# Idle transposes at both ends of the many-head cross attention of a 32-batch perceiver on one core

## What is computed

```python
x = x + _L2_xattn_ref(_layernorm(x, axis=-1), ctx_1024, ctx_1024, mask_1x1xSxS2_bk1,
                      L2_xattn_W_q, L2_xattn_W_k, L2_xattn_W_v, L2_xattn_W_o)

Q = _split(query @ W_q.T)
K = _split(key @ W_k.T)
V = _split(value @ W_v.T)
scores = jnp.einsum('bhqd,bhkd->bhqk', Q, K) / jnp.sqrt(jnp.float32(D_K))
scores = jnp.where(mask, -jnp.inf, scores)
attn_w = jax.nn.softmax(scores, axis=-1)
...
return merged @ W_o.T
```

## Time and profile before

| | us |
|---|---|
| median of 3 runs | 3170.89 (3170.31 to 3174.92) |
| the profiled execution | 3176.26 |
| its span, from the first to the last instruction | 3174.5 |
| mean granted clock of TensorE in it | 0.901 |
| PE busy | 2655.7 (84%) |
| DVE busy | 2031.4 (64%) |
| ACT busy | 1385.5 (44%) |

### The profile page before, as it was taken

The page is one execution under the profiler, slowest core; times in us unless marked ns, Lnnn a source line. Parts: engine busy times, 40 slices in busy tenths (PEclk is TensorE's granted clock), DMA queues, the critical chain, the costliest instruction groups (busy, mean ns, idle before and its releaser), DMA issues. The chain is left out here.

```text
span 3174.5 us, 65839 instructions
## 1 busy us (share of the span) xinstructions
PE 2655.7 (84%) x26678; PEld 1702.4 (54%) x26678; DVE 2031.4 (64%) x6795; ACT 1385.5 (44%) x2527; POOL 427.0 (13%) x299
## 2 busy tenths in 40 slices
PE   7989553796999699999999999999947989988433
PEld 5767442454666445665556556566524555655323
DVE  5554303576111259899989998998557876536776
ACT  3441211464333225555555555555338964335411
POOL 0000101341000000000000000000004950554100
PEclk9989786897999769999999999999768999899766
DMA  7960041000000100001000100010002210990000
GB/s 238 333 206 1 26 133 29 8 3 16 14 14 14 39 22 23 23 23 33 23 23 23 33 23 23 23 33 2 1 8 80 97 54 6 334 352 26 9 0 14
DMA packets 78239, 188.98 MB, mean 60 GB/s; under 512 B 12418, under 2 KB 46149, under 8 KB 77904
## 3 DMA queue, kind: packets, MB, share of 16 engines
q1 hardware_dynamic: 76912, 182.91, 17.5%
q0 software_dynamic: 1024, 1.85, 0.2%
HBM read 154.19 MB, written 30.79 MB: 58 GB/s over the span
## 5 line engine op out<-in xcount | busy, mean ns | idle before, releaser
L3031 DVE CUSTOM_DVE_ANT_0 L_xattn_junk<-L_xattn_ps_mx,L_xattn_shift 128x512 f32<-128x512 f32 (+1 forms) x1024 | 544.9, 570 | 127.3 <-issue 117.2
L3112 ACT ACTIVATE L_xattn_pT<-L_xattn_ps_st 128x512 f32<-128x512 f32 x768 | 416.9, 594 | 412.4 <-PE L_xattn_ps_st L2882 412.4
L2895 PE MATMUL L_xattn_ps_mx<-L_xattn_kT,L_xattn_qb 32*128 32x512 f32 (+1 forms) x2048 | 496.4, 567 | 1.8 <-DVE L_xattn_tops L3031 1.8
L2882 PE MATMUL L_xattn_ps_st<-L_xattn_qb,L_xattn_kT 32*128 32x256 f32 (+1 forms) x3328 | 463.4, 389 | 0.0
L3077 DVE TENSOR_TENSOR L_xattn_pT<-L_xattn_pT,L_xattn_capT 128x512 f32<-128x512 f32 (+1 forms) x704 | 419.3, 637 | 40.5 <-ACT L_xattn_pT L3112 37.8
L2882 PEld LDWEIGHTS L_xattn_ps_st<-L_xattn_qb,L_xattn_kT 32*128 32x128 f32 (+1 forms) x3328 | 304.1, 183 | 20.7 <-issue 1.2
L2942 PE MATMUL L_xattn_ps_pv<-L_xattn_pT,L_xattn_v 128*17 128x128 f32 x6656 | 267.7, 280 | 0.0
L2942 PEld LDWEIGHTS L_xattn_ps_pv<-L_xattn_pT,L_xattn_v 128*17 128x17 f32 x6656 | 148.4, 98 | 167.0 <-issue 81.0
L2908 PE MATMUL L_xattn_ps_st<-L_xattn_less,L_xattn_ones_b 3*128 3x512 bf16 x768 | 180.6, 390 | 1.4 <-ACT L_xattn_pT L3112 1.2
L1882 DVE SCALAR_TENSOR_TENSOR x<-L_ffn_ps_o,L_ffn_weights,x 128x128 f32<-128x128 f32 x128 | 36.1, 345 | 224.4 <-PE L_ffn_ps_o L1795 224.4
L2895 PEld LDWEIGHTS L_xattn_ps_mx<-L_xattn_kT,L_xattn_qb 32*128 32x128 f32 x2048 | 157.8, 188 | 36.0 <-DVE L_xattn_tops L3031 23.5
(11 more groups left out here) (611 smaller groups left out, 4974.5 us busy)
## 6 DMA issues: line engine op xcount, KB each, us to landing
L_xattn_ctxT<-context_turned SPq DMA_DIRECT2D x64, 800.5 KB, 5.9
L_xattn_ctx<-in_ctx SPq DMA_DIRECT2D x64, 768.0 KB
context_turned<-L_xattn_ctxT SPq DMA_DIRECT2D x32, 800.5 KB, 9.6
L_attn_cc<-scratch_rows SPq DMA_DIRECT2D x32, 512.0 KB, 3.7
L_ffn_w<-in_L_ffn_w SPq DMA_DIRECT2D x32, 256.0 KB, 3.2
L_xattn_out_keys<-scratch_q SPq DMA_DIRECT2D x32, 200.1 KB, 10.0
L_ffn_w<-in_L_ffn_W SPq DMA_DIRECT2D x16, 256.0 KB, 3.1
L_xattn_mask<-in_mask_pairs SPq DMA_DIRECT2D x32, 100.1 KB, 15.1
```

Source lines behind the costliest of these rows:

```text
L2882: last = nc.tensor.matmul(st[0:chunk[j], w % 3, 256 * c2:256 * c2 + 256], kT[n % 3][r:r + 32, P * j:P * j + chunk[j]], qb[n % 3][r:r + 32, ...
L2895: last = nc.tensor.matmul(mx[:, w % 3, to:to + width], qb[n % 3][32 * g:32 * g + 32, 2 * (p % 2):2 * (p % 2) + 2, :].rearrange("p h q -> p ...
L3031: last = nc.vector.tensor_tensor_reduce(out=junk[:, w % 3, to:to + width], in0=mx[:, w % 3, to:to + width], in1=shift[:, k0:k0 + width], s ...
L3112: nc.scalar.activation(pT[b % HELD][:, :, gi, :], st[:, w % 3, :].rearrange("p (c k) -> p c k", c=2), ACT.Exp)\
```

## The change

Three things, all in `many_head_cross_attention`. `masked_here` no longer names bundles from BUNDLES - LEAD = 430 on: the masks of bundles 438, 441 and 443 go from PE (line 2921) to DVE (line 3077), and the waits that count them follow, since all engines ask the same function. A new function on PE, `kept_busy`, called at the end of each iteration, transposes the identity into a part of a bank that nobody reads: 8 times in each of the 14 iterations before -18, 6 times in each of the 18 iterations -18 to -1 (into `st`, not in use before iteration 0), and 4 times in each of the 27 iterations 431 to 457 (into `mx`). Ahead of the last sort stands one new wait, in iteration 431, until DVE has taken all maxima out of `mx`.

```diff
-        masked_here = lambda b: b % ROUND in ON_TENSOR
+        masked_here = lambda b: b % ROUND in ON_TENSOR and b < BUNDLES - LEAD
...
+            def kept_busy(b):
+
+                if b < 0:
+                    for _ in range(8 if b < -LEAD else 6):
+                        nc.tensor.transpose(st[:, 2, 0:P], c.ident[:, :], c.ident[:, :])
+                elif b > BUNDLES - LEAD:
+                    if b == BUNDLES - LEAD + 1:
+                        pe.wait_ge(topped, 2 * BUNDLES)
+                    for _ in range(4):
+                        nc.tensor.transpose(mx[:, 0, 0:P], c.ident[:, :], c.ident[:, :])
+
             for b in range(FIRST, LAST):
...
                 prepare(early(b))
                 prepare(late(b))
+                kept_busy(b)
```

## The result

The change is faster, by less than forecast. Its median is 3154.2 us (7 runs, 3150.2 to 3162.5), and the ratio to the kernel before, run beside it (median 3177.4 us of 7), is 0.9936 (95% interval 0.9925 to 0.9946), which is 20 us; run once more later it was 0.9954 (0.9939 to 0.9969), 15 us. The forecast was 29.4 us. One slow execution of the kernel before (3692 us, mean granted clock 0.691) is left out of every comparison. The trace has a span of 3152.4 us in place of 3174.5, and its mean granted clock went from 0.901 to 0.921.

A forecast was written before the change was run, and what follows sets the result against it. TensorE at half clock was taken to bound both ends of the many-head stage. Terms of +2.5 - 15.2 - 1.2 - 15.5 = -29.4 us took the median from 3170.9 to 3141.5 us, range 3132 to 3157.

The forecast's parts named there:

- A: Both ends of the many-head stage run at full clock; 3141.5 us expected, 3133 to 3150, chance 0.80.
- D: In the fill the clock rises but falls again among the narrow maxima for some 20 us; 3156 us, chance 0.06.
- What bounds the two ends: Fill and drain of the many-head stage are set by TensorE at half clock, not by idleness; at most 57 us available.
- Fill, first part: Iterations -32 to -19, 8 transposes each: the clock rises after 3 to 6 us; 20.6 us against 18.1, costs 2.5.
- Fill, second part: Iterations -18 to -1, 6 transposes each, at full clock: 42.1 us against 57.3, saves 15.2.
- Start of the scores: -1.2 us: The 2.7 us at 0.50 behind the fill, until 1167.2, run at full clock and save 1.2 us.
- Drain: -15.5 us: Iterations 431 to 457: clock stays up, 18.0 us saved; transposes cost 4.1; moved masks save 1.6.
- Rival B: The drain's clock falls despite four transposes per iteration, while the fill keeps its 13.9 us gain; 3168.5 us, chance 0.08.
- Rival C: Identity transposes do not raise the clock in iterations -32 to -1; slower, 3195.9 us, or 3222.9 with drain low; chance 0.06.

The follow-up runs named there:

- the run with narrow work: The change with its idle fill transposes replaced by half as many idle float32 matmuls of 32 rows by 32 columns; the fill took 117.8 us, against 61.5.
- the best version: Against the change: transposes 8 per iteration in -32 to -29, 6 in -10 to -5, 1 in 418 to 424, 2 in 431 to 438; 3127.5 us, ratio 0.9873.
- the run with thin doses: Against the change: 8 transposes per iteration in -32 to -29, none to -19, 2 in -18 to -1, 1 in 412 to 430, 1 in 431 to 457; ratio 0.9959.

## Why the prediction was right or wrong, point by point

- *The number.* The median of 3154.2 us lies in the stated range of 3132 to 3157, but outside A's own 3133 to 3150 and next to D's 3156, and D's mechanism did not come: that it fits is in part luck. By the ratio to the kernel run beside it, the forecast's 3170.9 would have become 3150.6. The 29.4 us were missed by a third to a half, and by the points that follow.
- *What bounds the two ends.* Right. At full clock the fill took 13.9 us less although it carries 220 transposes more, and the 1.00 is there from 1087.1 on; the run with narrow work shows that it is not the filled gaps.
- *Fill, first part.* Forecast 20.6 us, measured 19.9 (1084.2 to 1104.1). The rise came 2.9 us after the first unit, 3.4 forecast.
- *Fill, second part.* Forecast 42.1, measured 41.7. Maxima, a unit and six transposes were forecast at 2.78 us and take 2.77 (1104.06 to 1106.83). In it the six take 0.75, not 0.66, and the unit ahead of them 0.96, not 1.06. DVE did not become the bound.
- *Start of the scores: -1.2 us.* The 2.7 us of low clock are gone, as forecast, but the term had to stand beside another that was not in the sum: the clock fell at 2213.5 for 10.2 us and the steady part came out 2.6 us longer. This is the first step that failed: the prediction read the steady part by its row from 1200 to 2200, at 1.00, and put what comes between it and the drain at nothing. Preparation ends with iteration 411, so from 412 on the stage is thinner than that row. With one transpose in each of seven iterations there the stretch is 1085.6 without a fall, against 1089.1, so the fall costs 3.5 us. That the thinning has its part is shown by one trace: the change with transposes there had no fall. The three later runs with one per iteration in all or some of it had none either, but they had fewer in the fill as well. What in the fill brings the fall on is not shown. All six traces with full-width transposes all through the second part of the fill and none behind 411 have it, and none of the three without any in the fill. Full clock in the fill is not the condition, since the narrow run, whose fill was at 0.50 throughout, had a fall of 3.4 us in the same place.
- *Drain: -15.5 us.* The mechanism was right, the size off: 10.3. The step that failed is the price of the transposes, "17 iterations to 447 x 0.24 = 4.1 us paid", with nothing for the tail. The wait of 0.20 us stands in an iteration with values of 65 rows (at 2261.3), and was taken off one that has none. Where an iteration has full values and no unit of preparation nothing was hidden, and a group of four costs 0.59, not 0.44; in most others 0.1 to 0.3 of it is hidden. What all of it comes to is shown by the run with two transposes in 431 to 438 and none behind, its clock at 1.00 up to 2267.1: its drain took 39.7 us against 48.1, so the 92 transposes that it leaves out cost 8.4. The last part, from the start of iteration 447 to the next stage, with the change and in that run:

```profile
2273.20:2282.90 9.70, 9.15 (x105) 6.58 (x105) 2.81 (x10) 0.65 (x2) 0.00 (x0) 1.00 0.01 2
```

```profile
2261.60:2268.20 6.60, 3.81 (x65) 2.16 (x62) 3.35 (x12) 0.74 (x3) 0.00 (x0) 0.92 0.01 2
```

  So 3.1 of the 8.4 us lie in the tail, where PE's waits for DVE were to hide them. With some 2 us for the other 16 (an estimate from 0.37 us for two, less what hides), the price is about 10.4 instead of 4.1. The masks gave 2.3 where 1.6 was forecast, which leaves 10.3 + 10.4 - 2.3 = 18.4 us for the clock, forecast at 18.0. The prediction's support for the clock staying up, "nothing but narrow tiles" for 11.8 us, was also misread: that stretch holds a turned M of 128x128 (at 2254.8).
- *Rival B* (the drain falls all the same) did not come, but it was near: with one transpose the clock falls, with two it does not. The prediction was wrong to say that the Trainium skill's rule of idle gaps would give this rival: taken as the prediction takes it elsewhere, the rule would have a drain without gaps at full clock, and the kernel before had 0.50 there. *Rival C* did not come: full-width transposes of the identity raised the clock, as in rows 4. *Rival D* named a fall among the maxima of the fill. The change has none there, but the runs with two or no transposes in that place do, at 1129.3 and 1120.2; the fall of the change came over 420 iterations later.
- *Outside the stage* the forecast had nothing. The code is the same in all kernels here, and yet the part behind took 864.2 to 871.6 us in 14 traces and the part ahead 1079.5 to 1089.1. The stage gained 21.6 us and the whole 20 and 15; for the best version 45.2 and 40. The part behind took 865.0, 866.6 and 865.6 us in the three kernels with a drain at 0.50 and no transposes in it. It took 868.6 to 871.6 in five of the seven with four per iteration and 865.9 and 867.7 in the other two. It took 864.2 to 866.2 in the three with two per iteration in all or part of the drain, and 869.5 in the one that lost the clock with one. Whether the drain has a hand in this stays open; no run was made for it.

Summed: fill -13.9 (forecast -12.7), steady +2.6 (-1.2), drain -10.3 (-15.5), outside about +2 to +7 (0). The drain's transposes are the larger part of the miss.

## What to carry to other kernels

Where the granted clock is low while PE is busy, look at what its work is, its width above all, and not at its gaps alone, and price the cure by the clock rows. Here a short full-width burst lifted it, and after that only the thin places needed help. Take an added instruction as hidden only where the very iteration that it goes into has the wait; here a wait seen in one sort of iteration was given to all seventeen, and the waits of the tail were taken to hide 40 transposes that cost 3.1 us. And treat every part of a pipeline in which one kind of work has ended as a stage end of its own, the last iterations before the visible drain too.

## What the runs showed of the hardware that was not expected

- 122.4 us of TensorE without any idle time, on tiles of 32 rows beside full ones, stayed at 1.2 GHz throughout, while 2.9 us of full-width units and transposes raised it to 2.4 GHz.
- The same work can run at either level, by what came ahead of it. With two transposes in 431 to 438 and none behind, iterations 439 to 445 ran at 1.00; with the masks moved and no transposes anywhere, the same iterations ran at 0.50, with the same instructions, and PE had no gap in either:

```profile
2246.60:2260.20 13.60, 13.60 (x188) 9.00 (x186) 9.32 (x19) 7.00 (x13) 0.00 (x0) 1.00 0.00 1
```

```profile
2268.90:2292.70 23.80, 23.80 (x187) 13.55 (x186) 9.25 (x19) 7.35 (x14) 0.00 (x0) 0.50 0.01 1
```

- A group of idle transposes costs 0.15 us beside its 0.11 us for each at 2.4 GHz (0.59 for four, 0.37 for two, at 2268.5 and 2268.7), so one group of four is cheaper than two of two (an estimate: 0.59 against 0.74). A single one, at 2241.6 in the run with thin doses, takes 0.26, which agrees.
- Stretches of the stage repeat to 0.1 us from trace to trace while whole executions of one kernel range over 20 us.
